# A four-layer vision block on one core: value products turned round, queues reordered at the ends of attention and head, and the quantile search rearranged

## The reference

```python
# layer 1, on a = layer norm of x over channels
channel = sigmoid(relu(mean(a) @ ca_w1.T + ca_b1) @ ca_w2.T + ca_b2)
spatial = sigmoid(conv3x3(a, sa_w) + sa_b)
relative = sigmoid(conv1x1(relu(conv1x1(a, tp_w1) + tp_b1), tp_w2) + tp_b2)
quantile = jnp.quantile(abs(a).reshape(16, -1), 0.85, axis=1)     # one number per image
mask = sigmoid((abs(a) - quantile * relative) * 10)
x = x + a * mask * channel * spatial
# layer 2: 8 experts, the best two of each token, GELU (mixture of experts)
# layer 3, attention on a = layer norm of x
k = softmax(Wk a + bk, over pixels); q = softmax(Wq a + bq, over pixels, 8 heads of 16)
v = Wv a + bv
context = k @ v.T                    # 16 x 16 per image
x = x + Wo (q.T @ context) + bo
# layer 4, the head: 8 experts, all used, weights softmax(mean over images of a @ Wr + br)
```

## Time and profile before

| what | us |
|---|---|
| runs of the kernel before: median, lowest, highest of 3 | 220.24, 217.92, 221.53 |
| the profiled execution: its own time | 219.29 |
| the profiled execution: span from the first to the last instruction | 217.4 |
| PE busy in the span | 191.6 (88%) |
| DVE, ACT, POOL busy | 140.8, 110.2, 73.9 |
| mean granted TensorE clock (1.00 is full speed) | 0.894 |

### The profile page before, as it was taken

The page is one execution under the profiler, slowest core; times in us unless marked ns, Lnnn a source line. Parts: engine busy times, 40 slices in busy tenths (PEclk is TensorE's granted clock), DMA queues, the critical chain, the costliest instruction groups (busy, mean ns, idle before and its releaser), DMA issues.

```text
span 217.4 us, 3515 instructions
## 1 busy us (share of the span) xinstructions
PE 191.6 (88%) x1281; PEld 84.5 (39%) x1281; DVE 140.8 (65%) x310; ACT 110.2 (51%) x182; POOL 73.9 (34%) x105
## 2 busy tenths in 40 slices
PE   6987878979899999999999899786969899999880
PEld 4315543266244232222245788332224354323120
DVE  2448779758658858888867948853355057474862
ACT  2198579203687864561047548624762655454000
POOL 7550194340670222333380575870304600000000
PEclk9999555557999999999999859999996799999998
DMA  6519256000000000000000000000000000202022
GB/s 181 141 51 136 44 161 252 0 3 0 0 0 5 0 3 0 0 3 0 0 0 5 0 0 3 0 3 0 2 0 0 0 3 0 51 0 51 2 48 48
DMA packets 5761, 6.50 MB, mean 30 GB/s; under 512 B 2008, under 2 KB 5368, under 8 KB 5616
## 3 DMA queue, kind: packets, MB, share of 16 engines
q1 hardware_dynamic: 5024, 5.62, 10.2%
q10 hardware_dynamic: 720, 0.66, 1.3%
HBM read 4.01 MB, written 1.05 MB: 23 GB/s over the span
## 4 chain that ended last, share of the span: by engine, by line
PE 59%; DVE 16%; ACT 10%; issue 6%; DMA 4%; POOL 2%; SPq 1%; DVEq 0%; ACTq 0%
PE ps L882 7%; PE ps L715 6%; PE ps L380 5%; PE ps L666 5%; PE ps L927 5%; PE ps L914 4%; PE ps L365 3%; DMA hidden_of_all_tokens<-hidden_of_all_tokens 3%; PE ps L772 2%; PE ps L587 2%; ACT hidden_of_all_tokens L390 2%; PE ps L431 2%; ACT hidden_of_all_tokens L1089 2%; PE ps L685 2%; DMA x_resid<-in_x 2%
## 5 line engine op out<-in xcount | busy, mean ns | idle before, releaser
L1678 DVE SCALAR_TENSOR_TENSOR gated_x<-ps,bn_shift_negated,hidden_of_all_tokens 128x512 f32<-128x512 f32 x32 | 22.5, 745 | 18.1 <-PE ps L917 17.7
L1185 ACT ACTIVATE hidden_of_all_tokens<-ps,bn_shift,bn_scale 128x512 f32<-128x512 f32 x32 | 23.1, 773 | 15.5 <-PE ps L882 15.5
L390 ACT ACTIVATE hidden_of_all_tokens<-ps,weights 128x512 f32<-128x512 f32 x16 | 10.9, 682 | 28.5 <-PE ps L380 27.8
L384 POOL TENSOR_TENSOR hidden_of_all_tokens<-hidden_of_all_tokens 128x512 f32<-128x512 f32 x16 | 17.8, 1122 | 20.9 <-DVE hidden_of_all_tokens L402 16.9
L1089 ACT ACTIVATE hidden_of_all_tokens<-ps,weights 128x512 f32<-128x512 f32 x32 | 19.9, 685 | 9.1 <-PE ps L666 8.9
L1530 DVE TENSOR_TENSOR hidden_of_all_tokens<-hidden_of_all_tokens,ps 128x512 f32<-128x512 f32 x32 | 20.5, 682 | 5.8 <-PE ps L685 5.7
L882 PE MATMUL ps<-x_normed,weights 64*64 64x512 f32 x128 | 22.3, 664 | 0.5 <-ACT hidden_of_all_tokens L1185 0.5
L409 DVE TENSOR_TENSOR x_normed<-hidden_of_all_tokens 128x512 f32<-128x512 f32 x16 | 11.3, 707 | 14.0 <-ACT hidden_of_all_tokens L392 13.8
L380 PE MATMUL ps<-hidden_of_all_tokens,weights 128*128 128x512 f32 x32 | 16.9, 627 | 1.8 <-POOL hidden_of_all_tokens L384 1.8
L927 PE MATMUL ps<-gated_x,weights 64*64 64x512 f32 x32 | 16.5, 595 | 2.0 <-DVE x_resid L1686 1.4
L666 PE MATMUL ps<-x_normed,weights 64*64 64x512 f32 x128 | 17.4, 612 | 1.0 <-ACT hidden_of_all_tokens L1089 1.0
(11 more groups left out here) (286 smaller groups left out, 399.6 us busy)
## 6 DMA issues: line engine op xcount, KB each, us to landing
weights<-in_weights SPq DMA_DIRECT2D x1, 2087.5 KB, 7.8
out_x<-x_resid SPq DMA_DIRECT2D x8, 128.0 KB, 2.4
hidden_of_all_tokens<-hidden_of_all_tokens SPq DMA_DIRECT2D x7, 128.0 KB, 3.8
x_resid<-in_x ACTq DMA_DIRECT2D x4, 128.0 KB, 3.3
x_resid<-in_x SPq DMA_DIRECT2D x4, 128.0 KB, 3.7
weights<-in_weights SPq DMA_DIRECT2D x1, 419.0 KB, 5.3
taps_shifted<-taps_padded SPq DMA_DIRECT2D x9, 18.1 KB
weights<-in_weights SPq DMA_DIRECT2D x1, 130.0 KB, 2.4
```

The costliest lines, as they stand in the source:

```text
L384: pool.tensor_tensor(SQ[:, cols(q)], XC[:, cols(q)], XC[:, cols(q)], ALU.mult).then_inc(sq_ready, 1)
L1185: act.activation(h1_tile(t), tile_of(t, Z1_BANK), ACT.Relu, bias=bn_c[:, p:p + 1], scale=bn_a[:, p:p + 1]).then_inc(h1_ready, 1)
L1678: dve.scalar_tensor_tensor(HW[:, t % PAIRS].rearrange("p (b n) -> p b n", n=N), tile_of(t, Z2_BANK).rearrange("p (b n) -> p b n", n=N), ne ...
```

## The change

Nothing that is computed for the output differs but for the counts of the search, which are taken of unrounded values; only the values from which the order statistics are picked are rounded. By place:

- **Search.** The transfers write to a second buffer `RAW`. The three rounds of counts read `RAW`. The rounding becomes two halves on VectorE (`rounded(0)` behind the first count, `rounded(1)` behind the second), and the window steps wait for both. PE's `hidden_of_tokens` is cut in two with the second `sample_count` between; the first `sum_full` goes ahead of `relative_thresholds`, the second ahead of `channel_weights`, the third ahead of `center_input(1)`. On ScalarE the second count goes ahead of the channel weights.
- **End of the search.** `gt8` and its spread product go ahead of the branch (and are repeated within it). `keep_clock` has one product ahead of the branch and three behind it, and none behind the spread. GpSimd's third product L1773 waits for the prepared values (L1357) and no longer for the pick; the fourth waits for `gt8`.
- **Norm n = 1.** The first copy goes ahead of the last mask product on VectorE.
- **Attention.** The value product takes the weights `wkv` as stationary and 256 moving columns: 8 products in four groups of PSUM rows, half of them behind the second quarter's keys and half behind the last; ScalarE copies them out, PE turns them (four turns), ScalarE copies them out again. `queries(1)` moves ahead of the third quarter's keys, `keys_scale(1)` ahead of the second `queries_max`, two exponentials of queries later on ScalarE.
- **End of attention.** The last `queries_store` goes ahead of the norm's first logarithm on ScalarE; the norm's first square ahead of the last `queries_norm` on GpSimd.
- **Head.** The router's product L903 goes ahead of `f_up(2)`, and `keep_clock` adds two products behind `f_up(2)`.

```diff
...
         QX, QT, SW, REL, AB, SQ, XC, RS = (HID[:, i * COLS:(i + 1) * COLS] for i in range(BH))
+        RAW = QX
...
         KT = AB[:, Q:2 * Q]
+        V_ROWS = SW[:, 0:Q]
         MB = AB[:, 1024:2048].rearrange("p (h b c) -> p h b c", h=HALVES, b=BH)
...
             g = b * HALVES * GROUP
-            return QT[g:g + HALVES * GROUP, :].rearrange("j (c n) -> j c n", c=C // GROUP), AB[:, b * N:(b + 1) * N]
+            return RAW[g:g + HALVES * GROUP, :].rearrange("j (c n) -> j c n", c=C // GROUP), AB[:, b * N:(b + 1) * N]
...
-            def hidden_of_tokens():
+            def hidden_of_tokens(images):
                 pe.wait_ge(t_ready, NQ)
-                for t in range(2 * BH):
+                for t in range(2 * images[0], 2 * images[-1] + 2):
                     last = pe.matmul(PS[:, 3, cols(t // 2, 8)], T[:, cols(t, P)], w("ca_w1"), start=t % 2 == 0, stop=t % 2 == 1)
-                last.then_inc(ca_ready, 1)
+                return last
...
             sample_count(0)
-            hidden_of_tokens()
+            hidden_of_tokens(range(4))
             sample_count(1)
-            relative_thresholds()
+            hidden_of_tokens(range(4, BH)).then_inc(ca_ready, 1)
             pe.wait_ge(group_ready, 1)
             sum_full(0)
+            relative_thresholds()
             channel_hidden(0)
+            sum_full(1)
             channel_weights(0)
             center_input(0)
-            sum_full(1)
+            sum_full(2)
             center_input(1)
-            sum_full(2)
             for q in range(3):
...
             pe.matmul(PS[0:1, 3, 0:1], w("ones"), fail[:, :], start=True, stop=True).then_inc(pick_spread, 1)
-            keep_clock(pe, WT, 0, 2)
+            def spread_quantile(n):
+                pe.wait_ge(gt_ready, n + 1)
+                pe.matmul(PS[:, 2, 0:BH], w("half_sel"), gt8[:, :], start=True, stop=True).then_inc(gt_spread, 1)
+            spread_quantile(0)
+            keep_clock(pe, WT, 0, 1)
             pe.wait_ge(branch_ready, 1)
...
                 pe.matmul(PS[:, 0, 0:2], group16[:, :], counts[:, :], start=True, stop=True).then_inc(tail_spread, 1)
-            keep_clock(pe, WT, 0, 2)
-            pe.wait_ge(gt_ready, 1)
-            pe.matmul(PS[:, 2, 0:BH], w("half_sel"), gt8[:, :], start=True, stop=True).then_inc(gt_spread, 1)
-            keep_clock(pe, WT, 0, 4)
+                spread_quantile(1)
+            keep_clock(pe, WT, 0, 3)
...
                     last.then_inc(k_ready, 1)
-                if q == 2:
+                    pe.wait_ge(ln_taken, 3 * NQ)
+                    for j in range(4):
+                        last = pe.matmul(PS[cols(j, 32), 3, cols(q // 2, N)], w("wkv", cols=slice(32, 64)), T[:, cols(2 * q - 2 + j, N)], start=True, stop=True)
+                if q == 1:
                     queries(1)
-            pe.wait_ge(ln_taken, 3 * NQ)
-            for t in range(16):
-                last = pe.matmul(PS[:, 3, cols(t, 32)], T[:, cols(t, P)], w("wkv", cols=slice(32, 64)), start=True, stop=True)
+            last.then_inc(v_ready, 1)
+            pe.wait_ge(v_out, 1)
+            for k in range(4):
+                last = pe.transpose(PS[:, 2, cols(k, P)], V_ROWS[:, cols(k, P)], w("ident"))
             last.then_inc(v_ready, 1)
...
-            pe.wait_ge(v_out, 1)
+            pe.wait_ge(v_out, 2)
             pe.wait_ge(kt_out, 2)
                 for jj in range(2):
-                    last = pe.matmul(PS[0:32, 2, cols(b, 32)], V[:, cols(2 * b + jj, 32)], KT[:, cols(4 * (2 * g + jj) + j, 32)], start=jj == 0, stop=jj == 1)
+                    last = pe.matmul(PS[0:32, 2, cols(b, 32)], V[:, cols(4 * (2 * g + jj) + j, 32)], KT[:, cols(4 * (2 * g + jj) + j, 32)], start=jj == 0, stop=jj == 1)
             last.then_inc(cx_ready, 1)
...
             f_route(3).then_inc(fl_ready, 1)
-            f_up(2)
             pe.wait_ge(fl_chain, 1)
             last.then_inc(fl_ready, 1)
+            f_up(2)
+            pe.wait_ge(ln_taken, 4 * NQ)
+            keep_clock(pe, WT, 3, 2)
...
                 with nc.allow_low_precision(reason="whole numbers up to 2048"):
-                    act.activation(SQ[:, 0:COLS - first], QT[:, first:COLS], ACT.Sigmoid, bias=at[:, n + 1:n + 2], scale=-1.0,
+                    act.activation(SQ[:, 0:COLS - first], RAW[:, first:COLS], ACT.Sigmoid, bias=at[:, n + 1:n + 2], scale=-1.0,
                                    accum_out=counts[:, 1:2]).then_inc(full_act, 1)
-            act.wait_ge(rounded_ready, 1)
+            act.wait_ge(q_in, 16 * BH)
             full_below(0)
             relative_threshold(0)
+            full_below(1)
             channel_hidden(0)
             channel_weights(0)
-            full_below(1)
             relative_threshold(1)
             act.wait_ge(low_ready, 1)
+            act.wait_ge(rounded_ready, 2)
             act.activation(SQ[:, :], QT[:, :], ACT.Sigmoid, bias=low[:, 0:1], scale=-1.0,
...
             queries_out(1)
+            act.wait_ge(v_ready, 1)
+            act.activation(V_ROWS, PS[:, 3], ACT.Copy).then_inc(v_out, 1)
             keys_exp(1)
             queries_out(2)
-            queries_exp(1)
-            act.wait_ge(v_ready, 1)
-            act.activation(V[:, :], PS[:, 3], ACT.Copy).then_inc(v_out, 1)
+            act.wait_ge(v_ready, 2)
+            act.activation(V[:, :], PS[:, 2], ACT.Copy).then_inc(v_out, 1)
             keys_out(0)
             keys_out(1)
+            queries_exp(1)
             queries_out(3)
-            queries_exp(2)
             act.wait_ge(cx_ready, 1)
             act.activation(CTX[:, :], PS[0:32, 2, 0:N], ACT.Identity, bias=vb[:, 0:1]).then_inc(cx_out, 1)
+            queries_exp(2)
             queries_store(0)
...
             queries_store(6)
+            queries_store(7)
             ln_act_rstd(act, 3, 0, 1)
-            queries_store(7)
             def f_h1(s, only=None):
...
                 dve.tensor_reduce(sampled2[:, 0:64], LESS[1].rearrange("p b l t -> p (b l) t"), AX_X, ALU.add).then_inc(sample_set, 1)
-            dve.wait_ge(q_in, 16 * BH)
-            dve.tensor_scalar(QT[:, :], QT[:, :], TOP, TOP, ALU.add, ALU.subtract).then_inc(rounded_ready, 1)
             dve.wait_ge(w2_in, 16)
...
+            def rounded(half):
+                c = cols(half, COLS // 2)
+                dve.tensor_scalar(QT[:, c], RAW[:, c], TOP, TOP, ALU.add, ALU.subtract).then_inc(rounded_ready, 1)
             def full_below(n):
                 with nc.allow_low_precision(reason="whole numbers up to 2048"):
-                    dve.tensor_scalar(XC[:, 0:last], QT[:, 0:last], at[:, t:t + 1], None, ALU.is_lt, ALU.add,
+                    dve.tensor_scalar(XC[:, 0:last], RAW[:, 0:last], at[:, t:t + 1], None, ALU.is_lt, ALU.add,
                                       accum_out=counts[:, 0:1]).then_inc(full_dve, 1)
-            dve.wait_ge(rounded_ready, 1)
+            dve.wait_ge(q_in, 16 * BH)
             full_below(0)
+            rounded(0)
             dve.wait_ge(full_sum, 1)
...
             full_below(1)
+            rounded(1)
             missed(1)
...
             pick.wait()
+            dve.wait_ge(rounded_ready, 2)
             pick(dve.scalar_tensor_tensor(XC[:, :], QT[:, :], high[:, 0:1], QT[:, :], ALU.is_lt, ALU.mult))
...
             pick(dve.scalar_tensor_tensor(gt[:, :], both[:, 1:2], W_HIGH, gt[:, :], ALU.mult, ALU.add))
+            pick.wait()
+            dve.tensor_scalar(gt8[:, :], w("gt_sel"), gt[:, 0:1], None, ALU.mult).then_inc(gt_ready, 1)
             dve.wait_ge(pick_spread, 3)
             dve.wait_ge(branch_ready, 1)
-            pick.wait()
...
                 dve.wait_ge(chain_v, 10)
-            dve.tensor_scalar(gt8[:, :], w("gt_sel"), gt[:, 0:1], None, ALU.mult).then_inc(gt_ready, 1)
+                dve.wait_ge(gt_spread, 1)
+                dve.tensor_scalar(gt8[:, :], w("gt_sel"), gt[:, 0:1], None, ALU.mult).then_inc(gt_ready, 1)
+                dve.wait_ge(gt_spread, 2)
             dve.wait_ge(gt_spread, 1)
...
                         dve.scalar_tensor_tensor(AB[:, c], REL[:, c], neg_gt[:, b:b + 1], AB[:, c], ALU.mult, ALU.add).then_inc(diff_ready, 1)
+                if q == NQ:
+                    ln_dve_copy(dve, 1, 0)
                 if q >= 1:
                     dve.tensor_tensor(U[:, cols(q - 1)], U[:, cols(q - 1)], AB[:, cols(q - 1)], ALU.mult).then_inc(gated_ready, 1)
-            ln_dve(dve, 1)
+            for q in range(1, NQ):
+                ln_dve_copy(dve, 1, q)
+            for q in range(NQ):
+                ln_dve_scale(dve, 1, q)
             top = pick
...
             keys_scale(0)
+            keys_scale(1)
             queries_max(1)
             queries_sum(0)
-            keys_scale(1)
             queries_max(2)
...
                 if q == 2:
-                    pool.wait_ge(pick_ready, 3)
+                    pool.wait_ge(pick_ready, 1)
+                if q == 3:
+                    pool.wait_ge(gt_ready, 1)
```

(3 more changed lines are left out.)

## The result

The changed kernel took 207.8 us (median of 4, 207.63 to 209.46) against 220.4 (217.92 to 221.53): a ratio of 0.948 with an interval of 0.940 to 0.956. Run again later, unaltered (u9), it took 209.97 (median of 6, 208.12 to 210.31). The forecast was 210.0. The kernel before ranges wider: of the 25 executions beside the later runs two took 213.2 and 214.0 us, at mean granted clocks of 0.931 and 0.923, the others 217.9 to 223.0 at 0.886 to 0.916, so for u5 to u12 medians alone are compared and no interval is given. Against the 214.0 alone, the 209.97 that ran beside it is 4.0 less.

A forecast was written before the change was run, and what follows sets the result against it. Bound by three half-clock troughs (search, attention, head start), with other limits in each place touched; 0.3 + 1.9 + 0 + 1.7 + 1.95 + 0.45 + 3.0 = 9.3 off 219.29 gives 210.0 us, range 206.5 to 215.5.

The forecast's parts named there:

- Search: Search up to the pick: 0.3 us won, between 0.6 lost and 1.6 won, since PE's queue holds the pick product.
- the 1.4 us for the prepared values: Search: VectorE's prepared values come about 1.4 us earlier, from an earlier first count less the roundings and a later third count.
- the rival of a whole queue: Search: VectorE's rounding waits until GpSimd's queue is empty, 8.4 us later, 6.4 on the path; 216.4 us, chance 0.06.
- Branch and copy: Spread ahead of the branch wins 1.9 us net; the norm's copy ahead of the last mask product wins 0.
- The 1.08: Round the branch: `gt8`'s 1.08 us taken as a wait for GpSimd's L1773; if the branch's own, the gain is 1.5.
- the 0.5 charged for dummies and clock: Behind the branch: 0.5 us lost, between 0 and 2.0, to three dummies ending late and gated products at half clock.
- Attention, first half: Wider value products and reordered queries and keys start the mask earlier: 1.7 us won, between 0 and 2.65.
- GpSimd's ring of 16 instructions: Attention from the mask on: GpSimd's ring of query tiles sets the pace, so the gain of 1.7 us is kept.
- End: End of attention: earlier last store and GpSimd's earlier first square win 1.95 us, between 1.2 and 2.4.
- Router: Start of the head: router's product no longer behind `f_up(2)`, 0.45 us won, between 0 and 0.5.
- Head clock: Head's start: `f_up(2)` and two dummies fill PE's wait for the softmax, the clock holds; 3.0 us won, between 0 and 3.4.
- The rival of a clock that stays down into the expert layer: PE stays at half clock from the search into the expert layer, about 12 us on the path; 222 us, chance 0.04.

The follow-up runs named there:

- u5: Changed kernel with the old start of the head (third `f_up` ahead of the router's logits products, no dummies behind it): 214.49 us.
- u12: Kernel before the change with only the new start of the head (third `f_up` behind the router's logits products, two dummies): 217.04 us.
- u3: Changed kernel with `gt8` and its spread product behind the branch again, eight dummies and GpSimd's old waits: 211.98 us, ratio 0.970.
- u7: Changed kernel with three more dummies in attention, two behind the heads' products and one ahead of the mixing products: 208.49 us.
- u1: Changed kernel with the old first half of attention put back (32 narrow value products, no turns, old key scaling order): 212.28 us, ratio 0.969.
- u4: Changed kernel with the old end of attention (last store behind the norm's logarithm and exponential, first square behind last `queries_norm`): 210.94 us, ratio 0.963.
- u2: Changed kernel with the old search (rounding ahead of the first count, old PE and ScalarE orders), spread still ahead of the branch: 209.89 us, ratio 0.958.
- u6: Changed kernel without the two dummies at the head's start, its new order kept: 214.74 us.
- u10: Changed kernel, PE's last two centring products behind pick and spread, GpSimd's fourth channel product behind the end of VectorE's preparation, two dummies not three: 208.32 us.
- u8: Changed kernel, PE's last two centring products behind pick and spread, GpSimd's fourth channel product behind a wait ending as VectorE's preparation starts: 210.27 us.
- u11: Changed kernel with the edits of u7 and u10 together: 208.70 us.

## Why the prediction was right

The forecast counts from a profiled execution, 219.29, and the profiled execution of the changed kernel took 209.46: 9.9 us of span for the 9.3 forecast. By the medians the gain is 12.6 in the first runs and 10.1 in the later ones. That the sum comes within 0.6 is luck in part: 0.54 of the 9.9 lies ahead of the first sample, and misses of -0.8 to +0.7 in the terms cancel. By its own terms, predicted and as the first pair of traces had them:
- **Search** 0.3, measured -0.48, and -0.7 to 0.3 over the executions. That PE's queue keeps the gain from the path was right for this pair (pick product 41.40, walked 41.1). It isn't the rule: in five of eight traces with this search the pick product follows VectorE's values by 0.28. The step that failed is the 1.4 us for the prepared values. Against the first sample the first count came 2.0 earlier, as forecast, but the preparation began only 0.65 earlier, since the rounds lost 1.4 where 0.6 was charged; its length was taken over at 2.35 and came to 3.24, behind GpSimd, and L1374 lost 0.28 more. The prediction looked for GpSimd at the roundings, which took 0.69 and 0.90; the rival of a whole queue (8.4 us) didn't come, but a wait for one instruction came elsewhere. The Trainium skill, "SBUF — State Buffer", section "Who interferes with whom", has it that a VectorE instruction with two inputs in SBUF contends with a GpSimd instruction that reads SBUF, and that `tensor_scalar` can enter the two-port forms; the traces agree (3.24 instead of 2.35, ending 2.14 to 2.15 after GpSimd's fourth product in each of the nine traces in which the two overlap; 1.19 instead of 0.22, ending 0.03 after GpSimd's). The prediction's "the first to issue" can't be read off the starts: the preparation is recorded at 33.82, GpSimd's fourth product at 33.88, and the preparation waited all the same.
- **Branch and copy** 1.9 + 0, measured 2.63 + 0.40. The 1.08 was GpSimd's, as taken (`gt8` 0.23); the 0.5 charged for dummies and clock didn't come. What the 0.40 behind the first difference is made of was not separated. It stays in u3, with the old branch and the old dummies, and in u5 and u7, whose clock is at half speed until 54.3 and 52.6 us, behind the first difference (49.24 and 47.36). That points to the copy ahead of the last mask product, which was put at 0; no run undoes it alone.
- **Attention, first half** 1.7, measured 2.09, by another way than walked. The mask gained 3.51, more than the 2.65 of the best case, and 1.42 was given back. The failing step is "From the mask on GpSimd's ring of 16 instructions sets the pace, so the gain is kept": with the fall moved into the mixing products the ring waited for them. Where the clock held, the term was 3.56; against the old attention of u12 it is 0.7 to 2.1. So the 1.7 came out near by luck: the size hangs on where the clock falls in either kernel. What the four turns of the values do to the clock no run separates: with them it fell here in three of nine traces, without them in all three (the kernel before, u1, u12).
- **End** 1.95, measured 2.03 (u4: 2.02), by the way that was walked. **Router** 0.45, measured 0.47, and 0.28 lost between `f_up` and the logits' copy (4.98 or 4.99 in three other traces, u1, u2 and u12; not explained).
- **Head clock** 3.0, measured 2.49, as in u12. Its mechanism was right, and shown by u5 and u6; its size depends on the trough that would have been there, 6.8 us long before, over 13 in u6.

The rival of a clock that stays down into the expert layer came in part, as a second fall: in u9 the clock is back at 50.7 us and falls again at 64.3. u6, u9 and u10 lose 2.3 us there, u1 and u8 0.8, other traces of the changed kernel nothing. The number of dummies alone doesn't decide it: u9 is the unaltered kernel, and u12, with the old eight, lost 0.9 to the kernel before there. Its cause stays open.

## What to carry to other kernels

Cost a moved VectorE instruction with the GpSimd instruction that will run beside it, not with its length from a place where GpSimd was idle; moving one of the two can pass the wait on to the next pair that meets (u10, u11). Where an engine's clock falls behind its waits, two cheap dummies in the wait can be worth more than the reordering round it; test them alone and both ways (u6, u12). Before a microsecond is put down to an edit, run the unaltered kernel again and compare stage by stage.

## What the runs showed that I had not expected

The clock can fall while PE is busy by its records. Windows of u9, at the start of the expert layer:

```profile
60.00:64.00 4.00, 4.00 (x49) 2.29 (x48) 2.46 (x9) 3.89 (x6) 1.03 (x6) 1.00 0.02 6
64.00:64.50 0.50, 0.50 (x6) 0.21 (x8) 0.43 (x3) 0.50 (x2) 0.00 (x0) 0.82 0.00 0
64.50:65.00 0.50, 0.50 (x8) 0.00 (x0) 0.47 (x2) 0.50 (x2) 0.00 (x0) 0.50 0.00 0
...
71.00:71.50 0.50, 0.50 (x11) 0.37 (x8) 0.00 (x0) 0.23 (x1) 0.00 (x0) 0.85 0.00 0
```

PE shows 4.00 of 4.00 us busy, then 1.2 GHz instead of 2.4 from 64.3 to 71.1. About half of those four us are the expert router's products with 8 moving columns, such as these:

```profile
60.96 1.06 PE L652 MATMUL ps<-weights,x_normed 64*128 64x8 f32 x16
```

The changed kernel's first trace has the same products at the same place, and its clock held; so the records ahead of the fall don't explain it, and the cause stays open. And VectorE's eight greatest of 2048 values (MAX8, 2.29 us) took as long beside GpSimd's product (36.25 to 37.29 in u10) as without it, where the 8-column multiplication had to wait (1.19 instead of 0.22).
